# Reordered waits, a minimum in place of a negated maximum, and a shorter last group in a three-stage decoder kernel

## The reference

```python
# stage A: self-attention in fixed point (16 heads of 64)
h = layernorm(x);  q, k, v = fxp(h @ w_qkv.T)          # fxp: clip to +-8, truncate to 1/4096
dots = fxp(q @ k.T / 8);  attn = fxp(softmax(dots));  o = fxp(attn @ v)
x = x + fxp(o @ w_proj.T + b_proj)
# stage B: cross-attention to ctx (128 rows of 128 numbers)
h = layernorm(x);  q = h @ Wq;  k = ctx @ Wk;  v = ctx @ Wv
x = x + softmax(q @ k.T / 8) @ v @ Wo + bo
# stage C: feed-forward with two experts, one base matrix and two low-rank parts (top_k = 2)
h = layernorm(x)
for e in (0, 1):
    x += top_v[e] * (relu(h @ wi.T + h @ A[e].T @ B[e].T) @ wo.T)
```

## Time and profile before

| what | value |
|---|---|
| median of 3 runs | 677.7 us (676.95, 677.70, 677.73) |
| the profiled execution, its own time | 676.35 us |
| its span (first to last instruction) | 674.3 us |
| PE busy | 647.4 us |
| DVE, ACT, POOL busy | 522.1, 416.2, 358.9 us |
| granted PE clock, mean over the span | 0.997 |

### The profile page before, as it was taken

How to read it: one execution, slowest core, us unless ns; L and a number is a source line. 1 busy time by engine, 2 the same in 40 slices (tenths; PEclk the granted TensorE clock), 3 DMA queues, 4 the chain that set the end, 5 groups by cost and what they waited for, 6 DMA issues and landing times.

```text
span 674.3 us, 16211 instructions
## 1 busy us (share of the span) xinstructions
PE 647.4 (96%) x5347; PEld 553.6 (82%) x5347; DVE 522.1 (77%) x1048; ACT 416.2 (62%) x1460; POOL 358.9 (53%) x762
## 2 busy tenths in 40 slices
PE   8899999999999999989999998999999998999997
PEld 4688888788887888777888887888888887888986
DVE  5888789788878888866777777877677757888886
ACT  3588788788868888776555566465555543434433
POOL 5995476655766676755486778455356632010110
PEclk9899999999999999999999999999999999999999
DMA  7944000000000000031100000000000000000000
GB/s 228 396 173 189 1 2 1 2 1 0 0 0 0 0 0 8 8 126 64 45 1 17 3 1 1 17 1 1 1 0 0 0 1 1 1 33 13 19 31 31
DMA packets 10404, 23.91 MB, mean 35 GB/s; under 512 B 1634, under 2 KB 6034, under 8 KB 9458
## 3 DMA queue, kind: packets, MB, share of 16 engines
q1 hardware_dynamic: 8050, 14.90, 6.4%
q0 software_dynamic: 1872, 7.87, 3.3%
q10 hardware_dynamic: 432, 0.52, 0.2%
HBM read 21.19 MB, written 2.10 MB: 35 GB/s over the span
## 4 chain that ended last, share of the span: by engine, by line
PE 49%; DVE 5%; ACT 3%; issue 3%; POOL 1%; DVEq 0%; ACTq 0%; POOLq 0%
PE bank L574 12%; PE bank L576 11%; PE bank L575 11%; PE bank L758 5%; PE bank L770 4%; PE bank L746 4%; PE bank L592 1%; PE bank L896 1%; DVE mx L1299 1%; PE bank L639 1%; DVE xnT_lo L1159 0%; DVE x_sb L1127 0%; DVE hid L1386 0%; POOL p_int L346 0%; ACT e_sb L1050 0%
## 5 line engine op out<-in xcount | busy, mean ns | idle before, releaser
L437 POOL TENSOR_SCALAR p_f<-e_sb,rsum 128x128 f32<-128x128 f32 x256 | 90.6, 376 | 100.9 <-DVE rsum L1341 100.9
L346 POOL TENSOR_SCALAR p_int<-e_sb,rsc 128x128 int16<-128x128 f32 x256 | 107.3, 437 | 6.3 <-issue 5.9
L1050 ACT ACTIVATE e_sb<-bank,neg_max 128x128 f32<-128x128 f32 x256 | 90.1, 385 | 4.4 <-DVE neg_max L1303 4.4
L947 ACT ACTIVATE sgn<-bank 128x512 bf16<-128x512 f32 x96 | 54.5, 605 | 36.5 <-PE bank L576 36.5
L962 ACT ACTIVATE e_sb<-si 128x128 f32<-128x128 int16 x256 | 76.1, 314 | 0.7 <-DVE si L1263 0.7
L1165 DVE SCALAR_TENSOR_TENSOR ri<-sgn,bank 128x512 int16<-128x512 bf16 x96 | 63.3, 684 | 13.6 <-ACT sgn L947 12.1
L1036 ACT COPY q_sb<-bank 128x512 f32<-128x512 f32 x32 | 18.8, 586 | 63.4 <-PE bank L576 63.4
L1050 ACT ACTIVATION_READ_ACCUMULATOR e_sb<-bank,neg_max 128x1 f32 x256 | 57.7, 225 | 0.0
L574 PE MATMUL bank<-xnT_hi,wqk_lo 128*128 128x512 f32 x128 | 53.5, 418 | 1.3 <-DVE ri L1165 1.3
L962 ACT ACTIVATION_READ_ACCUMULATOR e_sb<-si 128x1 f32 x256 | 52.6, 206 | 0.0
L341 POOL TENSOR_TENSOR rsc<-rsum,growth 128x8 f32<-128x8 f32 x32 | 7.0, 219 | 84.1 <-DVE rsum L1201 80.2
(11 more groups left out here) (158 smaller groups left out, 2195.9 us busy)
## 6 DMA issues: line engine op xcount, KB each, us to landing
wB_raw<-in_wB SPq DMA_DIRECT2D x1, 3072.0 KB, 14.5
wB_hi<-in_wB POOLq DMA_DIRECT2D x1, 3072.0 KB, 11.3
wqk_raw<-in_wqk SPq DMA_DIRECT2D x8, 256.0 KB, 6.2
out<-x_sb SPq DMA_DIRECT2D x8, 256.0 KB, 2.2
wqk_hi<-in_wqk POOLq DMA_DIRECT2D x7, 256.0 KB, 8.1
x_sb<-in_x SPq DMA_DIRECT2D x3, 512.0 KB, 19.8
wp_raw<-in_wp SPq DMA_DIRECT2D x1, 1024.0 KB, 14.3
wp_hi<-in_wp POOLq DMA_DIRECT2D x1, 1024.0 KB, 8.3
```

The costliest lines, as they stand in the source:

```text
L346: i = nc.gpsimd.tensor_scalar(p_int[:, half, t, :], e_sb[:, half, t, :], rsc[:, half, t:t + 1], -0.5, ALU.mult, ALU.add)
L437: i = nc.gpsimd.tensor_scalar(p_f[:, half, t, :], e_sb[:, half, t, :], rsum[:, half, t:t + 1], 0.0, ALU.mult, ALU.add)
L947: nc.scalar.activation(sgn[:, m % 2, :], proj_ps[m % 2][:, :], ACT.Sign).then_inc(a_sgn, 1)
L1050: last = nc.scalar.activation(e_sb[:, (s - 1) % 2, t, :], s_ps[hh][:, (t % 4) * P:(t % 4 + 1) * P], ACT.Exp, bias=neg_max[:, t:t + 1], sca ...
```

## The change

In stage A: POOL waits for the clips of slot 0 ahead of the fourth and fifth low part, and the nine later parts are spread 1, 2, 2, 2, 2 behind slots 0 to 4; `a_limited` of the second half goes ahead of `a_add_rows` of the first. In stage B: queries are stored negated and scaled by 1/8, the row minimum takes the place of the maximum and its negation; `inv_std` goes ahead of the products of `b_weights`, `norm_apply` goes to the front of DVE's slots 5 and 6; the attended rows' parts go ahead of the normed ones in slot 7; in slot 0 of groups 1 to 3 PE's first half of the output projection goes ahead of the transposes; some low parts and statistics of the first group move. From B to C: the low-rank tile and the first two `c_expert0` are made in the drain, the products of hidden block 2 and the first low-rank product stand ahead of the last output projection, ACT's copy of that projection stands behind the first hidden block's casts. In C: `hid` has two buffers, and the last group leaves out the statistics, transposes and parts of a norm that nothing reads.

```diff
     # gpsimd
-                if not first and s in (4, 5):
-                    a_add_rows(g, s - 4)
                 if not first and s == 4:
                     a_limited(g, 1)
+                if not first and s in (4, 5):
+                    a_add_rows(g, s - 4)
...
+            pool.wait_ge(a_clip, 2)
             for part in LOW_ORDER[3:5]:
                 make_low(*part)
...
-                if s < 4:
-                    for part in LOW_ORDER[5 + (0, 3, 5, 7)[s]:5 + (3, 5, 7, 9)[s]]:
+                if s < 5:
+                    for part in LOW_ORDER[5 + (0, 1, 3, 5, 7)[s]:5 + (1, 3, 5, 7, 9)[s]]:
                         make_low(*part)
...
             def b_slot(g, s, first=False, merging=False):
+                if s == 4:
+                    inv_std(G + g + 1)
                 if not (first and s == 0):
                     b_weights(NP * g + s - 1, (s - 1) % 2)
-                if s == 4:
-                    inv_std(G + g + 1)
     # tensor
                 if s == 0:
+                    if not first:
+                        project((0, 1))
                     transposes()
                     b_block(g, s, "q")
-                    project((0, 1))
+                    if first:
+                        project((0, 1))
...
+            def c_low_rank(g, p, n):
+                wait(pe, c_g0, n + 1)
+                if p == 0:
+                    wait(pe, c_tlo, g + 1)
+                pe.matmul(up_ps[p % 4][:, :], lb2T[:, p * P:(p + 1) * P], lowT[:, :], start=False, stop=True,
+                          skip_group_check=True).then_inc(c_u2, 1)
...
-                if not drain and s > (1 if first else 0):
+                if not drain and s > (2 if first else 0):
                     c_up(g, s)
-                if s == NF - 1:
+                if s == NF - 1 and not last:
                     normed_T(2 * G + g + 1, lambda: wait(pe, c_tlo, g + 1))
...
                 if s == 0 and first:
+                    pe.wait_ge(g_lb, 5)
+                    c_low_rank(0, 0, 0)
+                    c_up(0, 2)
                     b_slot(G, LAG, drain=True)
-                    pe.wait_ge(g_lb, 5)
     # scalar
-                    nc.scalar.copy(q_sb[:, s % 2, :], one_ps[:, :]).then_inc(b_q, 1)
+                    nc.scalar.activation(q_sb[:, s % 2, :], one_ps[:, :], ACT.Copy, scale=-DH ** -0.5).then_inc(b_q, 1)
...
-                        wait(act, b_nm, 2 * n - 1 + hh)
+                        wait(act, b_mx, 2 * n - 1 + hh)
...
-                                                        bias=neg_max[:, t:t + 1], scale=DH ** -0.5,
+                                                        bias=neg_max[:, t:t + 1], scale=-1.0,
...
-                if s == NP - 1 and not drain:
-                    xnT_high(G + g + 1)
...
                     nc.scalar.copy(oT_hi[:, :], o_ps[:, :]).then_inc(b_ohi, 1)
+                if s == NP - 1 and not drain:
+                    xnT_high(G + g + 1)
...
+                if first and s == 1:
+                    b_y_out(G)
     # vector
+                if not drain and s in (5, 6):
+                    norm_apply(G + g + 1, (g + 1) % G, (ln_T, 2 * (G + g) + 2), (0, 1) if s == 5 else (2, 3))
...
-                        V.reduce_max(mx[:, half], s_ps[hh][:, :].rearrange("p (a t) -> p a t", a=GB), AX).then_inc(b_mx, 1)
-                    for hh in range(2):
-                        half = slice(GB * hh, GB * hh + GB)
-                        wait(dve, b_mx, 2 * n - 1 + hh)
-                        V.tensor_scalar(neg_max[:, half], mx[:, half], -DH ** -0.5, None, ALU.mult).then_inc(b_nm, 1)
+                        V.tensor_reduce(neg_max[:, half], s_ps[hh][:, :].rearrange("p (a t) -> p a t", a=GB), AX,
+                                        ALU.min).then_inc(b_mx, 1)
+                if first and 1 <= s <= LAG:
+                    a_out_low(NP * G + s - 1 - LAG)
...
+                if drain and s == LAG - 1:
+                    for up in range(2):
+                        c_expert0(0, up, up)
...
-                    if s in (1, 3):
+                    if s in (1, 2 if first else 3):
                         norm_stats(G + g + 1, (g + 1) % G, (0, 1) if s == 1 else (2, 3))
...
-                if s == NP - 1:
-                    xnT_low(G + g + 1)
...
                     V.tensor_tensor(oT_lo[:, :], o_ps[:, :], oT_hi[:, :].bitcast(F32), ALU.subtract).then_inc(b_olo, 1)
+                if s == NP - 1:
+                    xnT_low(G + g + 1)
...
-                    wait(dve, c_glo, n - 1)
-                    V.scalar_tensor_tensor(hid[:, :], relu1[:, :], top_sb[:, 1:2], hid0[:, p % 2, :], ALU.mult,
+                    wait(dve, c_glo, n - 2)
+                    V.scalar_tensor_tensor(hid[:, p % 2, :], relu1[:, :], top_sb[:, 1:2], hid0[:, p % 2, :], ALU.mult,
```

More of the change, by code:

```diff
@@ L385, in a_slot @@
                     a_limited(g, 0)
+                if not first and s == 4:
+                    a_limited(g, 1)
                 if not first and s in (4, 5):
                     a_add_rows(g, s - 4)
-                if not first and s == 4:
-                    a_limited(g, 1)
                 if last and s == 6:
@@ L921, in _ @@
                 c_slot(0, s, first=True)
-            with pe.Fori(1, G) as g:
+            with pe.Fori(1, G - 1) as g:
                 for s in range(NF):
                     c_slot(g, s)
+            for s in range(NF):
+                c_slot(G - 1, s, last=True)
             for s in range(3):
@@ L1080, in _, with c_low_high, c_slot @@
                     b_slot(g, s)
+            def c_low_high(g):
+                wait(act, c_t, g + 1)
+                nc.scalar.copy(lowT[:, :], low_ps[0:96, :]).then_inc(c_thi, 1)
             for s in range(LAG):
                 b_slot(G, s, drain=True)
-            def c_slot(g, s, first=False, drain=False):
+                if s == 0:
+                    c_low_high(0)
+            def c_slot(g, s, first=False, last=False, drain=False):
                 n = NF * g + s
-                if s == NF - 1:
+                if s == NF - 1 and not last:
                     xnT_high(2 * G + g + 1)
@@ L1093, in c_slot @@
                     nc.scalar.activation(relu1[:, :], up_ps[p % 4][:, :], ACT.Relu).then_inc(c_r1, 1)
-                if s == 0 and not drain:
-                    wait(act, c_t, g + 1)
-                    nc.scalar.copy(lowT[:, :], low_ps[0:96, :]).then_inc(c_thi, 1)
-                    if first:
-                        b_y_out(G)
+                if s == 0 and not drain and not first:
+                    c_low_high(g)
                 if not (first and s < 1) and not (drain and s >= 1):
                     wait(act, c_g, n)
-                    if first and s == 1:
+                    if first and s == 2:
                         wait(act, b_pj, NP * G)
                     wait(act, c_dn, n - 2)
-                    nc.scalar.copy(tile_hi[p % 2][:, :], hid[:, :]).then_inc(c_ghi, 1)
+                    nc.scalar.copy(tile_hi[p % 2][:, :], hid[:, p % 2, :]).then_inc(c_ghi, 1)
+                if first and s == 1:
+                    b_y_out(G)
             for s in range(NF):
                 c_slot(0, s, first=True)
-            with act.Fori(1, G) as g:
+            with act.Fori(1, G - 1) as g:
                 for s in range(NF):
                     c_slot(g, s)
+            for s in range(NF):
+                c_slot(G - 1, s, last=True)
             c_slot(G, 0, drain=True)
@@ L1377, in c_slot @@
                     wait(dve, c_ghi, n - 1)
-                    V.tensor_tensor(tile_lo[p % 2][:, :], hid[:, :], tile_hi[p % 2][:, :].bitcast(F32),
+                    V.tensor_tensor(tile_lo[p % 2][:, :], hid[:, p % 2, :], tile_hi[p % 2][:, :].bitcast(F32),
                                     ALU.subtract).then_inc(c_glo, 1)
-                if s == NF - 1:
+                if s == NF - 1 and not last:
                     xnT_low(2 * G + g + 1)
@@ L1402, in c_slot @@
                     wait(dve, b_x, 2 * G)
-            def c_expert0(g, s, n):
-                wait(dve, c_u, n + 1)
-                wait(dve, c_g, n - 1)
-                V.tensor_scalar(hid0[:, s % 2, :], up_ps[s % 4][:, :], 0.0, top_sb[:, 0:1], ALU.max,
-                                ALU.mult).then_inc(c_g0, 1)
             for s in range(NF):
                 c_slot(0, s, first=True)
-            with dve.Fori(1, G) as g:
+            with dve.Fori(1, G - 1) as g:
                 for s in range(NF):
                     c_slot(g, s)
+            for s in range(NF):
+                c_slot(G - 1, s, last=True)
             for s in range(3):
```

58 lines of the change are left out of this document (29 added, 29 removed).

## The result

| | before | after |
|---|---|---|
| median, 4 runs each, same chip | 677.72 us (676.95 to 679.84) | 659.61 us (659.04 to 662.14) |
| ratio of after to before, 95% interval | | 0.9735 [0.9702, 0.9769] |
| the profiled execution, its own time | 676.35 us | 659.75 us |
| its span | 674.3 us | 657.7 us |
| PE's waits, sum of the list | 22.7 us | 10.3 us |

What follows compares the result with a forecast made beforehand. PE, busy 96% of the span, was taken to bound the kernel, so only its waits could go: 3.2 + 5.5 + 3.1 + 2.8 + 1.2 = 15.8 us, giving 660.5 from the profiled run, 661.9 from the median; forecast 661.5, range 657.5 to 667.5.

Steps and rivals of the forecast that it cites:

- The frame: Whole kernel: PE is busy 96% of the span, so with its work unchanged only its waits can be won back.
- Item 1: Start of stage A: faster clips, earlier scores of slot 1 and no clock fall give 3.2 us (bounds 1.0 and 4.3).
- Item 2: Group boundaries of stage A: DVE's wait for near goes, 1.85 us per group, 5.5 for three (bounds 3.0 to 5.9).
- Item 3: Stage B: shorter waits in group 0, group 1's slot 6 and at boundaries, 3.1 us (bounds 1.0 and 4.5).
- item 4: From B to C: two waits of PE go, less 0.5 us given back; gain 2.8 us (bounds 1.2 and 3.4).
- item 5: The end: the last group's transposes and DVE work ahead of the seventh hid go, 1.2 us (bounds 0.8 and 1.6).
- The zero terms: Stage B: inv_std, projection order and attended parts first each counted 0; the scaled query copy was put at 0.1 us.
- (a): Rival, stages A and B to C: starved conversions only move, the clock falls, DVE is late again; 667 us, 21%.
- (b): Rival: more comes back than counted, including the reordered projection and upper bounds at A's start and B to C; 658, 13%.
- (c): Rival, stage B: the scaled query copy needs another activation table, two loads in each of 32 slots; 700 us, 2%.
- (d): Rival: waits named are only the last releaser's, another holds PE as long; some 3 us gained, 674 us, 3%.

Runs made afterwards that it cites:

- experiment 1: Changed kernel with POOL's limiting of the second half again behind the addition of the first (stage A, groups 1 to 3): 669.45 us, ratio 0.9861.
- experiment 2: Changed kernel without POOL's wait for the clips of slot 0, new spacing of the low parts kept: 661.67 us, ratio 0.9757.
- experiment 3: Changed kernel with the old spacing of the low parts (3, 2, 2, 2 behind slots 0 to 3), wait for the clips kept: 665.79 us, ratio 0.9818.
- experiment 4: Changed kernel with the passage from B to C as before (order of PE, ACT and DVE), two hid buffers kept: 662.64 us, ratio 0.9814.
- experiment 5: Changed kernel with the projection's first half again between query and value block in slot 0 of stage B's groups 1 to 3: 660.23 us, ratio 0.9744.
- experiment 6: Changed kernel with norm_apply again behind the value rows in slots 5 and 6 of stage B: 660.51 us, ratio 0.9794.
- experiment 7: Changed kernel with the maximum and its negation in place of the minimum, queries copied unscaled (stage B): 663.13 us, ratio 0.9793.
- experiment 8: Changed kernel with one further edit, the query block ahead of the transposes in slot 0 of stage B's groups 1 to 3: 658.17 us, ratio 0.9713.
- experiment 12: Changed kernel with the last group's statistics, transposes and parts of an unread norm put back, two hid buffers kept: 660.32 us, ratio 0.9752.
- experiment 9: Changed kernel unaltered, six more runs: 659.10 us, ratio 0.9724.

## Why the prediction was right, and where its terms were off

**The frame** held. PE bounds the kernel, its work was left as it was, and the gain is the sum of its waits, measured from start to start. The profiled execution came out 0.8 us below the sum's own 660.5.

**Item 1** (3.2; 2.70). Its two parts came as worked out: slot 1's scores started 8.78 us after slot 0's before and 6.93 after, 1.85 less (1.95 forecast), and the clock that no longer fell gave 1.17 (1.25 forecast). The 0.5 us missing stand ahead of both, in slot 0, whose scores came 0.51 us later because their keys did (wait of 1.22 us in place of 0.85). The same kernel's other profiled run has 0.83 there, and experiments 1 to 8 and 12, which leave this place alone, 0.80 to 1.31, so I put that down to the run, not to the change. The clock's share holds for the two profiled runs. Of the 25 runs of the kernel before that the experiments brought, the ten with a mean clock of 1.000, in which it cannot have fallen as in the profiled one, have a median of 676.7 us, and the eleven with 0.996 or 0.997 one of 676.9. What the fall costs from run to run is thus not shown. What the item did not see is that the conversion that it gave a single price has two, below.

**Item 2** (5.5; 6.57, and 6.8 undone). The mechanism is shown by experiment 1. The size of a group's wait was 0.4 us too small, and the item came out above its upper bound of 5.9. The missing part is in the prediction's own words: it says that the matmul behind each wait also starts about 0.1 us late, but its 1.98 us for a group are the 1.50 us of idle and three times 0.16 alone. Three times 0.1 more make 2.3, what was measured. The fear that the rounding would suffer beside POOL's scaling did not come true.

**Item 3** (3.1; 2.44) has the right sum from partly wrong pieces. The step that failed is the claim that in a steady slot the removed scaling of the maxima hides. It does in the old order; in the changed order it no longer would, and experiment 7 prices it at 3.7 us. This is no gain over before, where those slots had no such wait, but a loss that one edit spared another: the parts of the change depend on each other, and costing them one by one could not show it. That `norm_apply` at the front of slots 5 and 6 is that other edit follows from where the loss stands; both undone together were not run. Group 0's slots 2 and 3 gave 1.2 us of the 1.3, and since experiment 7 leaves them alone, by elimination it is the reordering of stage A's last low parts and the statistics that gave them; that was not run by itself. `xn` gave 1.2 of 1.1 forecast (experiment 6: 1.1). The boundaries gave 0.2 in all instead of 0.7. The two 0.24 and 0.55 us at the value rows went as said, but the wait for the query copy took their place, 0.75 us at each.

**Items 4 and 5** (2.8; 3.05 and 1.2; 1.51) were right in place and size. The second `hid` took 1.52 us beside POOL's additions, as item 4 had it. Between the first down projection, which had gained 3.28 us, and the next transposes, at 3.05, 0.2 us were lost again, not the 0.5 given back for it. Of the end, experiment 12 shows 1.2. Another 0.3 was not forecast: PE's wait at the last down projection is 0.35 us in place of 0.56, and 0.1 went with the third of the waits for `x_sb` above; their cause was not tried.

**The zero terms.** The projection's order is worth 0 to -0.25 us (experiment 5). The query copy with a scale took 599 ns on average against 586. What the attended parts and `inv_std` did was not run by itself.

**The rivals.** (a), at 667, has the right mechanism and a smaller price: in the profiled run of experiment 9 the starved conversion did move to slot 1's queries, for 1.8 us of the 5.7. The run of 662.14 in the first set, mean clock 0.997, may be another; it was not profiled. (b), at 658, named the reordered projection, which gave nothing. (c) is refuted by the groups by line, which still show a single table load in the whole span:

```profile
L945 ACT ACT_TABLE_LOAD x1 | 1.3, 1283 | 2.1 <-issue 2.1
```

The Trainium skill (ScalarE: Activation LUTs, section "What ACT_TABLE_LOAD costs") gives 1283 ns for a load, as this row does; that negated queries with a scale need no second table is what the row shows by its count. (d) is refuted by the waits, whose sum fell by 12.4 us.

## What to carry to other kernels

Read a wait as the loss in start times, not as the idle time of its row: here 2.2 to 2.3 us stood behind rows that add up to 1.5. When an edit delays one engine's queue, look for the next consumer of what is queued behind, and reorder with it: against both together, the wait for the clips without the spacing costs 6 us, the spacing without the wait up to 3.6. And take small instructions off a shared queue even where they hide today, since the next reordering may set them beside work that starves them.

## What the runs showed of the hardware

- **One conversion, two prices, by when it starts.** In slot 1 the query conversion (128x512, int16 to f32) runs beside POOL's four subtractions. Where it started 1.52 to 1.56 us after the first of them, it took 1.54 to 1.58 us (experiments 1, 5, 8, 9). Where it started 1.78 to 1.79 us after (the changed kernel, experiments 3, 4, 7, 12; 1.77 in experiment 6), it took 0.62 to 0.64. In the latter POOL had sat waiting for the clips, in the former it came to its subtractions late and found them done. The keys behind it took 1.09 in the first case and 0.94 in the second. Why a quarter of a microsecond decides is not shown. With the scores' waits behind it (2.08 and 1.05 us in place of 1.07 and 0.24) the difference is 1.8 us of the whole time; with the clock's fall on top, 3.1.
- **DVE can lose to a series.** The Trainium skill (SBUF — State Buffer, section "SBUF: two separate sides") has the port pair that VectorE and GpSimd share locked for one whole instruction. As an estimate from that, two clips could lose at most two subtractions of 0.71 us, 1.4 in all. They lost 2.6 in the kernel before and in the profiled run of experiment 2 (3.12 us in place of 0.49). There the page and the trace differ: in the earlier trace rows the first clip alone took 2.41 us, though it began 0.12 us ahead of the first subtraction.
- **The clock and a wait.** In the profiled runs it fell to 1.2 GHz, for 3.4 us each time, 0.5 to 1.4 us after PE came out of waits of 2.68 us (before), 2.69 (experiment 2) and 2.08 (experiment 1). In experiment 3 it fell for 6.8 us, and that within the wait of 2.17 us, 1.25 us before its end. It stayed at 2.4 GHz behind a wait of 2.08 us at the same place in experiments 5, 8 and 9. In these rows the length of the wait alone does not decide.
- **Single long runs.** One run each of experiments 4 and 6 took 669.7 and 669.2 us, 7 and 9 above the rest, with mean clocks of 0.997 and 0.994. The kernel before has such runs too, 6 of 25 at 679.4 to 681.7. None of them was profiled, so what happened in them stays open.
